# Every second product of a selective scan made on GpSimd, three units ahead, in a fused decoder kernel

## The chip, the cores and the metric

One core of one Trainium2 chip runs the whole kernel in one launch. The metric is device time in microseconds (us), from the start of the program to its end, median of several runs. Engines: TensorE (PE in the profile; PEld is its weight load), VectorE (DVE), ScalarE (ACT), GpSimd (POOL) and SyncE (SP), which here issues the DMAs.

## The reference, cut to what matters

Two decoder layers over 16 sequences of 256 tokens with 256 features, all float32: a Mamba block, a latent sparse attention and a quantised feed-forward net, then a self-attention, a cross-attention and a mixture of experts, each with a residual and a layer norm. The change is in the scan of the Mamba block (512 inner features, 16 states):

```
def step(h, inp):
    dt_t, B_t, C_t, x_t = inp
    dA = jnp.exp(dt_t[..., None] * A)
    dBx = dt_t[..., None] * B_t[:, None, :] * x_t[..., None]
    h = dA * h + dBx
    y_t = jnp.sum(h * C_t[:, None, :], axis=-1)
    return (h, y_t)
```

## The kernel before, in words

The scan of a sequence is cut into 32 units. A unit has 128 partitions (16 features by 8 states) and two halves of the states side by side, 128 x 512 elements for the 256 tokens. For unit k:

- SyncE loads two rows spread over the partitions from a scratch in HBM: dt into `dt_rep[k % 8]`, and dt*x into `dtx_rep[k % 8]` (L331). A buffer is loaded again when its reader of eight units before is done.
- ScalarE makes the decay exp(dt*A) into PSUM (L1061, two instructions). PSUM has room for two units, so decay k waits for scan k-2.
- The product dt*x*B goes into `hbuf[k % 8]`. This is the product of the title. VectorE makes it one unit ahead of its scan (L1515, B read from PSUM), or GpSimd does (L1314, B read from its copy `bsb` in SBUF).
- VectorE scans in place (L1535).
- GpSimd multiplies by C in place (L1322); call it multiplication k.
- TensorE sums over the states for four units at a time (L552), and with that four buffers come free (`y_ps`).

Before the change GpSimd makes products 3, 7, ..., 31, five units ahead, and VectorE the others. After the scan of a sequence GpSimd adds the convolution of the next one (L1302), three instructions for each half.

Each engine has two streams of pieces: the x stream (`all_first`: scan, latent attention, feed-forward net) of sequence i+1 and the y stream (`all_second`: self-attention, cross-attention, experts) of sequence i. `merged` weaves them in an order written out by hand in `ORDER`; each `yield` ends a piece. A number of x pieces goes ahead first, so the first sequence scans with nothing beside it. GpSimd has the scan's work and the convolution alone.

Neighbours of the scan in the y stream that the prediction speaks of: the layer norm (L1396, L1397 and L1398, 128x2 elements, and L1403 twice, 128x256) at the end of the experts, in front of scan 0, and again behind the self-attention, in front of scan 24; the projections (L745) and key copies (L1173) of self-attention; its row maxima (L1558) and score matmuls (L608, L627); the key projections (L770), key copies (L1183) and value projections (L780) of cross-attention; the last matmul of the experts (L860) with the first of the feed-forward net (L698).

The order in which GpSimd works, before:

```
product(3)
for k in range(UNITS):
    if k % 4 == 2 and k + 5 < UNITS:
        product(k + 5)
    pool.wait_ge(h_ready, at(i, UNITS, k + 1))
    nc.gpsimd.tensor_tensor(hbuf[k % HSLOTS], hbuf[k % HSLOTS],
                            csb, ALU.mult).then_inc(hc_ready, 1)
```

Of the kernel before, what the change touches and what calls it, by code (L numbers as in the profile page):

```python
# [51 lines left out]
def at(i, per, n):  # L52

    return i * per + n
# [65 lines left out]
def build(nc, dram, out):  # L120

    ctx = ExitStack()
    with ctx:
# [197 lines left out]
        def _(sp):  # L321
# [31 lines left out]
            def first_half(i):  # L353
# [10 lines left out]
                for k in range(UNITS):  # L364
# [10 lines left out]
                    if k == 4:  # L375
                        sp.wait_ge(cnt_ps, at(i, 4, 4))
                    if k >= SLOTS and k % 4 == 3:
                        sp.wait_ge(dbx_pool, at(i, UNITS // 4, (k - SLOTS) // 4 + 1))
                    elif k >= SLOTS:
                        sp.wait_ge(dbx, at(i, 24, (k - SLOTS) // 4 * 3 + k % 4 + 1))  # L380
                    if k == 0 or k == UNITS // 2:
# [9 lines left out]
                sp.wait_ge(decay_ready, at(i, UNITS, UNITS))  # L391
                sp.wait_ge(dbx, at(i, 24, 24))
                sp.wait_ge(dbx_pool, at(i, UNITS // 4, UNITS // 4))
                for row, name in ((fb1, "fb1"), (ln2g, "ln2g"), (ln2b, "ln2b")):
# [898 lines left out]
        def _(pool):  # L1293
# [11 lines left out]
            for i in range(B):  # L1305
                pool.wait_ge(c_sb, i + 1)

                def product(k):
                    if k == 3:
                        pool.wait_ge(dbx, at(i, 24, 1))  # L1310
                    elif k >= HSLOTS:
                        pool.wait_ge(y_ps, at(i, 8, k // 4 - 1))
                    pool.wait_ge(rep_dtx[k % SLOTS], at(i, 64, 16 * (k // SLOTS + 1)))
                    nc.gpsimd.tensor_tensor(hbuf[k % HSLOTS], dtx_rep[k % SLOTS].unsqueeze(1).to_broadcast([P, 2, T]), bsb,  # L1314
                                            ALU.mult).then_inc(dbx_pool, 1)

                product(3)
                for k in range(UNITS):
                    if k % 4 == 2 and k + 5 < UNITS:
                        product(k + 5)  # L1320
                    pool.wait_ge(h_ready, at(i, UNITS, k + 1))
# [6 lines left out]
        def _(v):  # L1328
# [154 lines left out]
            def mamba(i, c, before, dt_steps):  # L1483
# [25 lines left out]
                def product(k):  # L1509
                    if k % 4 == 3:  # L1510
                        return
# [10 lines left out]
                for k in range(UNITS):  # L1522
# [4 lines left out]
                    if k + 1 < UNITS:  # L1527
                        product(k + 1)
                        yield
                    if k % 4 == 3:  # L1530
                        v.wait_ge(dbx_pool, at(i, UNITS // 4, k // 4 + 1))
                    else:
                        v.wait_ge(dbx, at(i, 24, k // 4 * 3 + k % 4 + 1))
                    v.wait_ge(decay_ready, at(i, UNITS, k + 1))
# [339 lines left out]
```

## Time and profile before

| | |
|---|---|
| median of 3 runs | 3829.47 us (3828.81 to 3829.94) |
| profiled execution | 3828.33 us, its span 3826.5 us |
| TensorE busy | 3238.3 us (85%), weight loads 2244.7 (59%) |
| VectorE busy | 2824.9 us (74%) |
| ScalarE busy | 2083.5 us (54%) |
| GpSimd busy | 923.2 us (24%) |
| mean granted TensorE clock | 0.932 |

The span runs from the first to the last instruction of the program; the profiled execution's own time has 1.8 us more around it. Busy shares are averages over stages with different limits, so the timeline of a stage says more than they do. A row of the timeline gives start, duration, engine, line, operation, result and inputs with their shapes and the number of instructions put together (x2), and in brackets how long the engine stood idle before it and what ended that.

### The profile page before, as it was taken

The page shows a single profiled execution, that of the slowest core. Times are in us where ns is not written, and L with a number is a line of the kernel's source. Part 1 is how long each engine was busy: PE and PEld are TensorE (multiplying, and loading weights), DVE is VectorE, ACT ScalarE, POOL GpSimd, SP SyncE. Part 2 cuts the span into 40 slices and gives each one's busy share as a digit, 9 for nine tenths or more (in the row PEclk, how much of TensorE's full clock was granted, in tenths as well). Part 3 has the DMA queues.
Part 4 walks back from the last instruction along what each step waited for, and adds up shares of the span by engine and source line. Part 5 has one row for each costly group of instructions (what it writes and reads, how often), then busy time and mean ns, then how long its engine had stood idle before and what let it go on. Part 6 is the DMA issues. An engine that isn't in the chain of part 4 may idle for free.

```text
span 3826.5 us, 58993 instructions
## 1 busy us (share of the span) xinstructions
PE 3238.3 (85%) x22354; PEld 2244.7 (59%) x22402; DVE 2824.9 (74%) x4915; ACT 2083.5 (54%) x4816; POOL 923.2 (24%) x740
## 2 busy tenths in 40 slices
PE   2568989898898989889898998989889888988877
PEld 2245656666565666656556665656656566665655
DVE  4687786868778687777868778786877868687622
ACT  2356555565665556556564655656566565655432
POOL 1423050221404122150411305031230503124000
PEclk8679999999999999999999999999999999999988
DMA  5212041412304132140413215041320504132110
GB/s 185 81 60 93 24 142 48 144 70 80 134 15 149 51 135 79 54 157 17 149 51 127 87 41 170 17 145 56 123 91 31 168 29 139 61 114 94 47 42 17
DMA packets 205692, 336.50 MB, mean 88 GB/s; under 512 B 23968, under 2 KB 175008, under 8 KB 190688
## 3 DMA queue, kind: packets, MB, share of 16 engines
q1 hardware_dynamic: 205408, 332.72, 25.5%
q8 instruction: 177, 2.90, 0.3%
q14 instruction: 107, 0.88, 0.1%
HBM read 311.66 MB, written 20.97 MB: 87 GB/s over the span
## 4 chain that ended last, share of the span: by engine, by line
PE 60%; DVE 21%; ACT 13%; issue 5%; DMA 1%; SPq 0%; POOL 0%; DVEq 0%; ACTq 0%
PE ps L627 7%; PE ps L608 5%; PE ps L860 4%; PE ps L940 4%; DVE nm L1558 3%; PE ps L639 3%; PE ps L794 3%; PE ps L780 3%; PE ps L770 3%; PE ps L879 3%; PE ps L825 3%; PE ps L745 3%; PE ps L806 2%; PE ps L552 2%; PE ps L839 2%
## 5 line engine op out<-in xcount | busy, mean ns | idle before, releaser
L1322 POOL TENSOR_TENSOR region_x<-region_x 128x512 f32<-128x512 f32 x512 | 645.6, 1273 | 340.3 <-DVE region_x L1535 340.0
L1535 DVE TENSOR_TENSOR_SCAN region_x<-ps,region_x 128x512 f32<-128x512 f32 x512 | 614.8, 1214 | 68.6 <-ACT ps L1061 65.6
L1061 ACT ACTIVATE ps<-region_x,aneg 128x255 f32<-128x255 f32 x1024 | 441.7, 473 | 348.2 <-DVE region_x L1535 341.4
L1302 POOL TENSOR_TENSOR region_x<-region_x 128x512 f32<-128x512 f32 x96 | 122.5, 1276 | 1209.8 <-ACT region_x L1009 1204.8
L1314 POOL TENSOR_TENSOR region_x<-region_x 128x512 f32<-128x512 f32 x128 | 162.5, 1270 | 1030.7 <-DVE region_x L1515 894.2
L1558 DVE TENSOR_REDUCE nm<-ps 128x4 f32<-128x1024 f32 x256 | 308.8, 1222 | 65.8 <-PE ps L608 57.6
L879 PE MATMUL ps<-xTy,wide 128*128 128x256 f32 x1280 | 310.7, 391 | 1.5 <-DVE region_y L1722 1.3
L1210 ACT ACTIVATE region_y<-ps,rmax 128x256 f32<-128x256 f32 x512 | 236.0, 495 | 116.7 <-DVE rmax L1663 116.7
L1515 DVE TENSOR_TENSOR region_x<-region_x,ps 128x512 f32<-128x512 f32 x384 | 254.6, 667 | 20.5 <-PE ps L552 20.3
L879 PEld LDWEIGHTS ps<-xTy,wide 128*128 128x128 f32 x1280 | 237.6, 192 | 41.1 <-issue 8.7
L1571 DVE SCALAR_TENSOR_TENSOR region_x<-region_x,cntk 128x512 f32<-128x512 f32 x256 | 168.5, 690 | 114.6 <-ACT region_x L1102 114.6
L1663 DVE TENSOR_REDUCE rmax<-ps 128x4 f32<-128x1024 f32 x128 | 152.2, 1220 | 116.0 <-PE ps L806 116.0
L627 PE MATMUL ps<-region_y 64*128 64x256 f32 x1024 | 179.0, 477 | 64.2 <-ACT region_y L1102 35.8
L608 PE MATMUL ps<-region_y 64*128 64x256 f32 x1024 | 145.5, 412 | 74.3 <-DVE nm L1558 34.8
L1226 ACT ACTIVATE region_y<-ps 128x512 f32<-128x512 f32 x256 | 142.3, 599 | 103.2 <-PE ps L828 103.2
L552 PE MATMUL ps<-region_x,sely 128*32 128x256 f32 x2048 | 153.8, 429 | 47.6 <-POOL region_x L1322 47.6
L1102 ACT ACTIVATE region_x<-ps 128x512 f32<-128x512 f32 x256 | 145.3, 605 | 78.8 <-PE ps L627 78.7
L627 PEld LDWEIGHTS ps<-region_y 64*128 64x128 f32 x1024 | 106.1, 224 | 136.1 <-ACT region_y L1102 93.8
L1102 ACT ACTIVATE region_y<-ps 128x512 f32<-128x512 f32 x256 | 138.5, 593 | 75.3 <-PE ps L627 75.1
L1412 DVE TENSOR_TENSOR xh<-ps,xh 128x512 f32<-128x512 f32 x80 | 55.0, 687 | 160.6 <-PE ps L669 56.6
L608 PEld LDWEIGHTS ps<-region_y 64*128 64x128 f32 x1024 | 93.2, 194 | 126.6 <-DVE nm L1558 66.7
L975 ACT ACT_TABLE_LOAD x127 | 162.9, 1283 | 3.0 <-PEq L1864 0.7
(249 smaller groups left out, 6913.3 us busy)
## 6 DMA issues: line engine op xcount, KB each, us to landing
region_x<-rows_of_dt SPq DMA_DIRECT2D x1024, 128.0 KB, 2.9
wide<-in_wgate SPq DMA_DIRECT2D x16, 1280.0 KB, 7.2
wide<-in_wup SPq DMA_DIRECT2D x16, 1280.0 KB, 10.1
down<-in_wmoe SPq DMA_DIRECT2D x16, 1280.0 KB, 5.5
wide<-in_wq SPq DMA_DIRECT2D x16, 1024.0 KB, 7.0
wide<-in_wk SPq DMA_DIRECT2D x16, 1024.0 KB, 8.8
wide<-in_wv SPq DMA_DIRECT2D x16, 1024.0 KB, 10.6
down<-in_wo SPq DMA_DIRECT2D x16, 1024.0 KB, 13.2
```

The costliest lines, as they stand in the source:

```text
L552: last = mm(bank(0)[32 * j:32 * j + 32, m, :], W["sely"][:, e, :], hbuf[(4 * n + j) % HSLOTS][:, half, :], start=(e + half == 0), stop=(e ...
L608: last = mm(ps[:, b + j, qt * T:(qt + 1) * T], a.QT[r, t, qt * P:(qt + 1) * P], a.KT[u % 2][r, t, :], start=not a.masked, stop=not a.maske ...
L627: last = mm(ps[:, a.sT_bank(n + j), kt * T:(kt + 1) * T], a.KT[e][r, t, kt * P:(kt + 1) * P], a.QT[r, t, :], start=True, stop=True)
L879: last = mm(bank(b)[:, j, :], w[:, k, f * P:(f + 1) * P], xTy[:, k, :], start=(k == 0), stop=(k == KD - 1))
L1061: last = f(ps[:, 1 + 2 * (k % 2), half * T + 1:(half + 1) * T], dt_rep[k % SLOTS][:, 1:T], ACT.Exp, scale=aneg[:, k, half:half + 1])
L1102: f(a.PT[:, n % 8].rearrange("p k q -> p (k q)"), ps[:, a.sT_bank(n), :], ACT.Exp).then_inc(a.probs, 1)
L1210: last = f(junk2[:, 4 * (u % 2) + 2 * qt + g], ps[:, a.pair_bank(u) + g, qt * T:(qt + 1) * T], ACT.Exp, bias=rmax[:, qt, g, u:u + 1], accu ...
L1322: nc.gpsimd.tensor_tensor(hbuf[k % HSLOTS], hbuf[k % HSLOTS], csb, ALU.mult).then_inc(hc_ready, 1)
L1515: tt_(hbuf[k % HSLOTS], dtx_rep[k % SLOTS].unsqueeze(1).to_broadcast([P, 2, T]), bank(2), ALU.mult).then_inc(dbx, 1)
L1535: nc.vector.tensor_tensor_scan(flat(hbuf[k % HSLOTS]), ps[:, 1 + 2 * (k % 2), :], flat(hbuf[k % HSLOTS]), 0.0, ALU.mult, ALU.add).then_inc ...
L1558: last = nc.vector.tensor_reduce(at_nm[:, u % 2::2, :, 16 + t], ps[:, b:b + 2, :].rearrange("p g (q k) -> p g q k", k=T), AX, ALU.max, neg ...
L1571: stt(a.PT[:, n % 8], a.PT[:, n % 8], 4.0, cntk[:], ALU.min, ALU.mult).then_inc(a.weighed, 1)
```

## The change

GpSimd makes products 1, 3, 5, ..., 31 and VectorE products 0, 2, 4, ..., 30. GpSimd starts with product 1, and makes product k+3 in front of multiplication k for each even k. The counts behind the semaphores `dbx` (VectorE's products) and `dbx_pool` (GpSimd's) become 16 a sequence each, and SyncE's and VectorE's waits go by them. The order of pieces is the same; where VectorE has no product to make, its piece is empty.

```
--- before.py
+++ after.py
@@ -374,10 +374,10 @@
                     yield
                     if k == 4:
                         sp.wait_ge(cnt_ps, at(i, 4, 4))
-                    if k >= SLOTS and k % 4 == 3:
-                        sp.wait_ge(dbx_pool, at(i, UNITS // 4, (k - SLOTS) // 4 + 1))
+                    if k >= SLOTS and k % 2 == 1:
+                        sp.wait_ge(dbx_pool, at(i, UNITS // 2, (k - SLOTS) // 2 + 1))
                     elif k >= SLOTS:
-                        sp.wait_ge(dbx, at(i, 24, (k - SLOTS) // 4 * 3 + k % 4 + 1))
+                        sp.wait_ge(dbx, at(i, UNITS // 2, (k - SLOTS) // 2 + 1))
                     if k == 0 or k == UNITS // 2:
                         sp.wait_ge(dt_stored[1], at(i, 32, 16 if k == 0 else 32))
                     spread_rows(i, 1, k, dtx_rep[k % SLOTS]).then_inc(rep_dtx[k % SLOTS], 16)
@@ -389,8 +389,8 @@
                             load_x(i)
                 yield
                 sp.wait_ge(decay_ready, at(i, UNITS, UNITS))
-                sp.wait_ge(dbx, at(i, 24, 24))
-                sp.wait_ge(dbx_pool, at(i, UNITS // 4, UNITS // 4))
+                sp.wait_ge(dbx, at(i, UNITS // 2, UNITS // 2))
+                sp.wait_ge(dbx_pool, at(i, UNITS // 2, UNITS // 2))
                 for row, name in ((fb1, "fb1"), (ln2g, "ln2g"), (ln2b, "ln2b")):
                     sp.dma_start(row, dram[name]).then_inc(rows_loaded, 16)
                 yield
@@ -1306,18 +1306,18 @@
                 pool.wait_ge(c_sb, i + 1)
 
                 def product(k):
-                    if k == 3:
-                        pool.wait_ge(dbx, at(i, 24, 1))
+                    if k == 1:
+                        pool.wait_ge(dbx, at(i, UNITS // 2, 1))
                     elif k >= HSLOTS:
                         pool.wait_ge(y_ps, at(i, 8, k // 4 - 1))
                     pool.wait_ge(rep_dtx[k % SLOTS], at(i, 64, 16 * (k // SLOTS + 1)))
                     nc.gpsimd.tensor_tensor(hbuf[k % HSLOTS], dtx_rep[k % SLOTS].unsqueeze(1).to_broadcast([P, 2, T]), bsb,
                                             ALU.mult).then_inc(dbx_pool, 1)
 
-                product(3)
+                product(1)
                 for k in range(UNITS):
-                    if k % 4 == 2 and k + 5 < UNITS:
-                        product(k + 5)
+                    if k % 2 == 0 and k + 3 < UNITS:
+                        product(k + 3)
                     pool.wait_ge(h_ready, at(i, UNITS, k + 1))
                     nc.gpsimd.tensor_tensor(hbuf[k % HSLOTS], hbuf[k % HSLOTS],
                                             csb, ALU.mult).then_inc(hc_ready, 1)
@@ -1507,7 +1507,7 @@
                     tt_(yT[:, 2 * pair:2 * pair + 2, :], zs[:, 2 * pair:2 * pair + 2, :], y, ALU.mult).then_inc(y_done, 1)
 
                 def product(k):
-                    if k % 4 == 3:
+                    if k % 2 == 1:
                         return
                     v.wait_ge(rep_dtx[k % SLOTS], at(i, 64, 16 * (k // SLOTS + 1)))
                     if k >= HSLOTS and k % 4 == 0:
@@ -1527,10 +1527,10 @@
                     if k + 1 < UNITS:
                         product(k + 1)
                         yield
-                    if k % 4 == 3:
-                        v.wait_ge(dbx_pool, at(i, UNITS // 4, k // 4 + 1))
+                    if k % 2 == 1:
+                        v.wait_ge(dbx_pool, at(i, UNITS // 2, k // 2 + 1))
                     else:
-                        v.wait_ge(dbx, at(i, 24, k // 4 * 3 + k % 4 + 1))
+                        v.wait_ge(dbx, at(i, UNITS // 2, k // 2 + 1))
                     v.wait_ge(decay_ready, at(i, UNITS, k + 1))
                     nc.vector.tensor_tensor_scan(flat(hbuf[k % HSLOTS]), ps[:, 1 + 2 * (k % 2), :], flat(hbuf[k % HSLOTS]),
                                                  0.0, ALU.mult, ALU.add).then_inc(h_ready, 1)
```

## Rows read from the trace of the kernel before

**Rows 1.** The page's chain that ended last, shares of the span by engine.

```profile
PE 60%; DVE 21%; ACT 13%; issue 5%; DMA 1%; SPq 0%; POOL 0%; DVEq 0%; ACTq 0%
```

**Rows 2.** The page's groups of products: count, busy us, mean ns, idle before.

```profile
L1314 POOL TENSOR_TENSOR region_x<-region_x 128x512 f32<-128x512 f32 x128 | 162.5, 1270 | 1030.7 <-DVE region_x L1515 894.2
...
L1515 DVE TENSOR_TENSOR region_x<-region_x,ps 128x512 f32<-128x512 f32 x384 | 254.6, 667 | 20.5 <-PE ps L552 20.3
```

**Rows 3.** Timeline of the first sequence's scan, GpSimd and TensorE.

```profile
87.63 1.27 POOL L1314 TENSOR_TENSOR region_x<-region_x 128x512 f32<-128x512 f32 x1 [19.69 <-DMA region_x<-rows_of_dt]
88.86 2.49 POOL L1322 TENSOR_TENSOR region_x<-region_x 128x512 f32<-128x512 f32 x2
...
94.62 4.95 POOL L1322 TENSOR_TENSOR region_x<-region_x 128x512 f32<-128x512 f32 x4
...
141.17 1.93 PE L552 MATMUL ps<-region_x,sely 128*32 128x256 f32 x16 [3.08 <-POOL region_x L1322]
```

**Rows 4.** Timeline of VectorE beside the convolution adds of GpSimd.

```profile
1774.63 3.96 POOL L1302 TENSOR_TENSOR region_x<-region_x 128x512 f32<-128x512 f32 x3 [72.44 <-ACT region_x L1009]
...
1775.01 0.92 DVE L1396 SCALAR_TENSOR_TENSOR x_nt<-x_mv,x_rstd 128x2 f32<-128x2 f32 x1 [0.24 <-ACT x_rstd L988]
...
1781.48 0.29 DVE L1431 TENSOR_SCALAR region_x<-region_x 128x256 bf16<-128x256 f32 x1
...
1782.40 1.34 DVE L1431 TENSOR_SCALAR region_x<-region_x 128x256 bf16<-128x256 f32 x1
```

**Rows 5.** Timeline of the start of the ninth sequence's scan, GpSimd and VectorE.

```profile
1847.10 1.27 POOL L1314 TENSOR_TENSOR region_x<-region_x 128x512 f32<-128x512 f32 x1 [60.76 <-DVE region_x L1515]
...
1847.48 0.90 DVE L1396 SCALAR_TENSOR_TENSOR y_nt<-y_mv,y_rstd 128x2 f32<-128x2 f32 x1
...
1848.81 0.74 DVE L1403 TENSOR_SCALAR xh<-xh,y_mv,y_rstd 128x256 f32<-128x256 f32 x2
...
1849.46 1.22 DVE L1535 TENSOR_TENSOR_SCAN region_x<-ps,region_x 128x512 f32<-128x512 f32 x1
```

**Rows 6.** Timeline in front of the key copies L1173.

```profile
1854.25 3.62 PE L745 MATMUL ps<-xTy,wk 128*128 128x256 f32 x16
...
1857.02 0.87 ACT L1061 ACTIVATE ps<-region_x,aneg 128x255 f32<-128x255 f32 x2 [0.84 <-DVE region_x L1535]
...
1857.91 3.76 ACT L1173 ACTIVATE region_y<-ps,kbp,hmp 128x256 f32<-128x256 f32 x8
```

**Rows 7.** The chain among the row maxima: start, us, what.

```profile
1867.17 0.68 DVE region_x L1515
```

**Rows 8.** Timeline around the second layer norm, in front of scan 24.

```profile
1907.91 2.50 POOL L1322 TENSOR_TENSOR region_x<-region_x 128x512 f32<-128x512 f32 x2
...
1910.44 0.16 DVE L1396 SCALAR_TENSOR_TENSOR y_nt<-y_mv,y_rstd 128x2 f32<-128x2 f32 x1
...
1913.00 0.87 ACT L1061 ACTIVATE ps<-region_x,aneg 128x255 f32<-128x255 f32 x2 [1.33 <-DVE region_x L1535]
...
1913.81 1.06 ACT L1183 ACTIVATE region_y<-ps 128x512 f32<-128x512 f32 x2
...
1914.68 0.30 PEld L780 LDWEIGHTS ps<-wide,ctxT 128*128 128x128 f32 x2 [0.41 <-ACT region_y L1183]
```

**Rows 9.** Timeline: first scans of the 14th and 15th sequence.

```profile
2976.12 1.22 DVE L1535 TENSOR_TENSOR_SCAN region_x<-ps,region_x 128x512 f32<-128x512 f32 x1
...
3201.14 1.22 DVE L1535 TENSOR_TENSOR_SCAN region_x<-ps,region_x 128x512 f32<-128x512 f32 x1
```

**Rows 10.** Timeline of TensorE at L860, in two sequences.

```profile
1783.98 6.10 PE L860 MATMUL ps<-down,region_y 128*128 128x256 f32 x16
1790.14 1.67 PE L698 MATMUL ps<-w1q,region_x 128*128 128x512 bf16 x7
...
2009.12 6.17 PE L860 MATMUL ps<-down,region_y 128*128 128x256 f32 x16
2015.35 1.67 PE L698 MATMUL ps<-w1q,region_x 128*128 128x512 bf16 x7
```

More of the change, by code:

```diff
@@ L376, in first_half @@
                         sp.wait_ge(cnt_ps, at(i, 4, 4))
-                    if k >= SLOTS and k % 4 == 3:
-                        sp.wait_ge(dbx_pool, at(i, UNITS // 4, (k - SLOTS) // 4 + 1))
+                    if k >= SLOTS and k % 2 == 1:
+                        sp.wait_ge(dbx_pool, at(i, UNITS // 2, (k - SLOTS) // 2 + 1))
                     elif k >= SLOTS:
-                        sp.wait_ge(dbx, at(i, 24, (k - SLOTS) // 4 * 3 + k % 4 + 1))
+                        sp.wait_ge(dbx, at(i, UNITS // 2, (k - SLOTS) // 2 + 1))
                     if k == 0 or k == UNITS // 2:
@@ L391, in first_half @@
                 sp.wait_ge(decay_ready, at(i, UNITS, UNITS))
-                sp.wait_ge(dbx, at(i, 24, 24))
-                sp.wait_ge(dbx_pool, at(i, UNITS // 4, UNITS // 4))
+                sp.wait_ge(dbx, at(i, UNITS // 2, UNITS // 2))
+                sp.wait_ge(dbx_pool, at(i, UNITS // 2, UNITS // 2))
                 for row, name in ((fb1, "fb1"), (ln2g, "ln2g"), (ln2b, "ln2b")):
@@ L1308, in product @@
                 def product(k):
-                    if k == 3:
-                        pool.wait_ge(dbx, at(i, 24, 1))
+                    if k == 1:
+                        pool.wait_ge(dbx, at(i, UNITS // 2, 1))
                     elif k >= HSLOTS:
@@ L1315, in product @@
                                             ALU.mult).then_inc(dbx_pool, 1)
-                product(3)
+                product(1)
                 for k in range(UNITS):
-                    if k % 4 == 2 and k + 5 < UNITS:
-                        product(k + 5)
+                    if k % 2 == 0 and k + 3 < UNITS:
+                        product(k + 3)
                     pool.wait_ge(h_ready, at(i, UNITS, k + 1))
@@ L1509, in product @@
                 def product(k):
-                    if k % 4 == 3:
+                    if k % 2 == 1:
                         return
@@ L1529, in mamba @@
                         yield
-                    if k % 4 == 3:
-                        v.wait_ge(dbx_pool, at(i, UNITS // 4, k // 4 + 1))
+                    if k % 2 == 1:
+                        v.wait_ge(dbx_pool, at(i, UNITS // 2, k // 2 + 1))
                     else:
-                        v.wait_ge(dbx, at(i, 24, k // 4 * 3 + k % 4 + 1))
+                        v.wait_ge(dbx, at(i, UNITS // 2, k // 2 + 1))
                     v.wait_ge(decay_ready, at(i, UNITS, k + 1))
```

## The prediction

> **What bounds the kernel now.** I read the chain that ended last first. TensorE has 60% of it, VectorE 21%, ScalarE 13%, GpSimd 0% [rows 1]. So moving VectorE work to GpSimd can gain only where VectorE is on that chain, and can lose where GpSimd or what it disturbs gets onto it. The groups then give the prices: a product costs 667 ns on VectorE and 1270 ns on GpSimd [rows 2], a scan 1.22 us [rows 5]. Products and scans of one unit after another start closer together than that; I use 0.57 to 0.60 us as what a product takes out of VectorE's time where neighbours overlap.
>
> The timeline shows two regimes. The first sequence scans alone, and there GpSimd works almost without a pause; TensorE's last sum at 141.17 waits for it [rows 3]. From the second sequence on, the scan of one sequence is woven with the attention of the sequence before, and everything repeats: from the first scan at 1849.46 to that at 3201.14 are 1351.68 us, which is six times 225.28 us [rows 5, 9].
>
> **The change part by part.** Products 1, 5, ..., 29 of each sequence go from VectorE to GpSimd: 8 x 16 = 128 instructions. VectorE loses 128 x 0.667 = 85 us of work, GpSimd gains 128 x 1.270 = 163 us [rows 2]. Every product on GpSimd now stands three units ahead of its scan instead of five. SyncE's waits before the row loads follow the products; those of the moved products come no later than before, so I cost them at nothing, hidden by the eight row buffers; with that cover gone each load would add its 2.9 us.
>
> First sequence. Before, GpSimd starts the first multiplication by C at 88.86, behind product 3 [rows 3]. After, products 1 and 3 are both done by then, since product 3 starts at 87.63 only because its rows land then. What is left from 88.86 is 32 multiplications and 14 products, 46 instructions. Back to back they start 1.227 us apart (four took 4.95: (4.95 - 1.27) / 3) [rows 3]. 88.86 + 46 x 1.227 = 145.3, against 141.1 where TensorE's last sum starts now. VectorE's two units take at most 3.1 us then (two scans and one product: 2 x 1.22 + 0.67), GpSimd's 3.68, so GpSimd is the bound and its products are what the scans wait for. Loss: 4.2 us, all of it on the chain, since nothing else runs in this sequence. Bounds: 0, if later work of the sequence hid it; 5.5 with one more product of 1.27 exposed.
>
> Beginning of each later sequence. A small VectorE instruction that reads two tensors from SBUF waits while GpSimd runs an instruction: beside the convolution adds of GpSimd the 128x2 operation L1396 took 0.92 us, and of two equal tensor_scalar operations, L1431, one took 0.29 us and the next 1.34 [rows 4]; with GpSimd idle L1396 takes 0.16 [rows 8]. At the start of the scan the last layer norm of the other sequence (L1396 to L1403) is followed by scan 0. Before, L1396 already waits for product 3 on GpSimd: 0.90 us, and ends at 1848.38, with GpSimd's instruction [rows 5]. After, GpSimd runs products 1 and 3 one behind the other, from 1847.1 to 1849.6, so one of these small operations waits for the first and another for the second. With L1403 (0.74 us for the pair) still to come, scan 0 starts at about 1850.35 instead of 1849.46: 0.9 us late, though VectorE has a product less before it. No row shows L1403 beside a busy GpSimd; I let it wait, by the row of L1431. If it doesn't wait, scan 0 is not late, which is the other bound. The skill says which VectorE instructions are meant: by the Trainium skill, GPSIMD Engine Reference, section 8 (Key points), the two engines share their SBUF interfaces, and those in a 2-port mode or with two SBUF inputs contend. By it the scan and the product, which each read PSUM and one SBUF tensor, pay nothing for the 128 new neighbours.
>
> The delay goes on to ScalarE: scans 0 to 4 release decay 6, behind which the key copies L1173 are queued. Without product 5 the path from scan 0 is 0.57 shorter. Decay 6 ended at 1857.89, TensorE's own input to L1173 came at 1857.87, and L1173 started at 1857.91 [rows 6]: both paths are full. After: 0.9 - 0.57 = +0.33 us on the chain (bounds 0 and 0.9; a gain is excluded, since TensorE's 1857.87 does not move).
>
> Row-maximum stretch. Here eight row maxima (L1558) share VectorE with the scans. At 1867.17 product 9 stands in the chain with 0.68 us [rows 7]. It goes: -0.58 us (bounds -0.68 and 0). GpSimd has it long before scan 9, which comes some 9 us behind it.
>
> Second layer norm. Units 20 to 23: GpSimd ran multiplications 22 and 23 from 1907.91 to 1910.41, then stood idle, and L1396 started at 1910.44 and took 0.16 [rows 8]. After, product 25 takes the place of 27 in front of these two, and product 27 starts behind them at 1910.4, before multiplication 24. L1396 or L1397 waits for it until 1911.65: scan 24 starts 1.05 us late. ScalarE's decay 26 waits for scan 24 (1913.00, idle 1.33 for VectorE), and the key copies L1183 are queued behind it. TensorE's value projection L780 at 1914.68 waits for these copies [rows 8]. They were ready at 1914.4 and come 1.05 later, TensorE goes on about 0.73 us late (bounds 0 and 1.1). From there to the sequence's end the chain is on TensorE. The other moved products (13, 17, 21) leave VectorE where it then waits for ScalarE or TensorE: nothing.
>
> Sum for one later sequence: +0.33 - 0.58 + 0.73 = +0.48 us.
>
> **What the repetition does with it.** It need not add up. The first scan at 2976.12 came 0.26 us behind the beat (1849.46 + 5 x 225.28 = 2975.86), the next sequence's, at 3201.14, stood exactly on it [rows 9]: a delay was given back within one sequence. The rows show one place where: L860 started at 1783.98, which is 0.14 behind its place by the next sequence (2009.12 - 225.28 = 1783.84), and L698 behind it at 1790.14 only 0.07 behind (2015.35 - 225.28 = 1790.07) [rows 10]. This happens in a stretch at the lower of TensorE's clocks (16 multiplications took 6.1 us): what starts later has less of its work left in it. A standing extra of 0.48 a sequence is absorbed in the same way, and only a standing lag of some 0.5 to 0.9 us is left at the end. I take 0.6.
>
> Forecast: 4.2 + 0.6 = 4.8 us. The profiled execution had 3828.33 us around a span of 3826.5; that gives 3833.1. Its time is 1.1 below the median of 3829.47, so a median of 3834.3; I say 3834. The change is 0.12%, and a measurement of this kernel can tell about 0.2% (7.7 us) from no change.
>
> **Rivals.**
> - The extra is not given back (slower). 15 x 0.48 = 7.2, with 4.2 it makes 11.4: 3841, +0.3%. It decides from 0.24 us a sequence on. For it: each term has its row. Against: rows 9. Chance 0.22.
> - The small operations wait no longer than now, and product 9's time counts each time: 4.2 - 15 x 0.58 = -4.5, 3825. For it: L1403's wait is shown by no row. Against: two products in a row are longer than one. Chance 0.14.
> - TensorE's first stretch at the lower clock falls elsewhere and VectorE's path is freed of products 1, 5 and 9: 4.2 - 15 x (0.58 + 1.15) = -21.8, 3808. For it: the lag moves TensorE's work. Against: L1173 also has ScalarE's path, full as it is. Chance 0.08.
> - GpSimd becomes the bound in every sequence, as in the first: 16 x 4.2 = 67, 3897. Against: in the later ones it stands idle in between, as from 1910.41 until scan 24 is done [rows 8]. Chance 0.07. The Trainium skill, GPSIMD Engine Reference, section 4.1 (Engine selection), speaks for this one, since it sends elementwise work on tiles to VectorE and calls GpSimd about twice as slow with two inputs; the rows agree on the ratio (1270 to 667).
> - The forecast, around 3834 (3828 to 3838): 0.49.
>
> **How the numbers follow.** Faster by over 0.2%: the third rival and the edge of the second, 0.1. Slower: the first, the fourth and the forecast's edge, 0.3. The same: 0.6. The range leaves out the third and fourth and reaches from below the second to behind the first with its bounds (15 x 0.9 = 13.5 with the 4.2): 3820 to 3847.
>
> **What would show it.** Right: in the first sequence the last L1322 ends near 145.3 and has next to no idle time; 256 products on each engine; L1396 to L1403 at the start of a scan together about 0.9 us longer; L1396 or L1397 near scan 24 at 1.1 to 1.3 us; sequences still 225.28 us apart. Wrong: another distance between sequences, which multiplies by 15, or stretches at the lower clock in other places; or L1535 waiting for L1314.

## The result, and the profile after

The changed kernel took 3855.64 us (median of 4, 3853.51 to 3857.13), the kernel before 3829.14 us (median of 4): ratio 1.0075, 95% interval 1.0063 to 1.0086. It is 0.75% slower. The forecast was 3834, with a range up to 3847: the measured time lies behind the range, and a difference that this measurement tells from none was forecast as one that it could not. The profiled execution had 3853.51 us around a span of 3851.5.

The page, chain by engine and four of its groups (line, engine, operation, count; busy us, mean ns; idle time before, and what ended it):

```profile
span 3851.5 us, 59089 instructions
...
PE 59%; DVE 20%; ACT 13%; issue 5%; POOL 1%; SPq 0%; DMA 0%; DVEq 0%; ACTq 0%
...
L1535 DVE TENSOR_TENSOR_SCAN region_x<-ps,region_x 128x512 f32<-128x512 f32 x512 | 610.3, 1210 | 99.6 <-ACT ps L1061 97.2
...
L1314 POOL TENSOR_TENSOR region_x<-region_x 128x512 f32<-128x512 f32 x256 | 324.9, 1271 | 1002.7 <-DVE region_x L1515 916.2
...
L627 PE MATMUL ps<-region_y 64*128 64x256 f32 x1024 | 193.7, 510 | 62.3 <-ACT region_y L1102 33.9
...
L1515 DVE TENSOR_TENSOR region_x<-region_x,ps 128x512 f32<-128x512 f32 x256 | 170.2, 665 | 28.3 <-PE ps L552 28.0
```

The work moved as foreseen: 256 products on each engine, 128 fewer on VectorE, each at its old price [rows 2]. The chain's shares are nearly those of [rows 1]; GpSimd has only 1% of it. Of the 99.6 us that VectorE stands idle ahead of its scans (L1535), 97.2 end with ScalarE's decay and next to none with GpSimd's products. So neither more work nor a new bound explains 25 us.

The timeline, first scans of the ninth, 14th and 15th sequence (start us, us, what):

```profile
1861.11 1.21 DVE L1535 TENSOR_TENSOR_SCAN region_x<-ps,region_x 128x512 f32<-128x512 f32 x1
...
2996.11 1.21 DVE L1535 TENSOR_TENSOR_SCAN region_x<-ps,region_x 128x512 f32<-128x512 f32 x1
...
3223.02 1.21 DVE L1535 TENSOR_TENSOR_SCAN region_x<-ps,region_x 128x512 f32<-128x512 f32 x1
```

From 1861.11 to 3223.02 are 1361.91 us, six times 226.99, where [rows 5, 9] had six times 225.28. That is the loss. From the end of TensorE's last instruction of the experts (L940) in the first sequence (491.85 before and after to 0.03) to the same in the 14th, the kernel now needs 2952.31 us instead of 2929.06; the rest behind it is 1.74 longer: 23.25 + 1.74 = 25.0 us of span.

**First sequence.** GpSimd, then TensorE's last sum:

```profile
85.35 1.26 POOL L1314 TENSOR_TENSOR region_x<-region_x 128x512 f32<-128x512 f32 x1 [0.80 <-DMA region_x<-rows_of_dt]
86.57 2.49 POOL L1322 TENSOR_TENSOR region_x<-region_x 128x512 f32<-128x512 f32 x2
...
143.23 1.93 PE L552 MATMUL ps<-region_x,sely 128*32 128x256 f32 x16 [4.18 <-POOL region_x L1322]
```

The rate was right: 86.57 + 46 x 1.227 = 143.0. The first multiplication stands 2.3 us earlier than in [rows 3], of which 1.9 is the start of this execution: SyncE's first stores of dt (L325) stand at 76.03 against 77.95, ahead of anything that the change touches. So TensorE's last sum is 2.06 us late, and 4.0 against its own start (forecast 4.2). At the end of the first sequence's experts both executions stand at the same place.

**Start of a later scan.** The same place as [rows 5]:

```profile
1858.01 0.15 DVE L1396 SCALAR_TENSOR_TENSOR y_nt<-y_mv,y_rstd 128x2 f32<-128x2 f32 x1
1858.20 0.16 DVE L1397 SCALAR_TENSOR_TENSOR y_nt<-y_nt,y_rstd 128x2 f32<-128x2 f32 x1
1858.23 2.49 POOL L1314 TENSOR_TENSOR region_x<-region_x 128x512 f32<-128x512 f32 x2 [60.62 <-DVE region_x L1515]
...
1858.39 1.12 DVE L1398 SCALAR_TENSOR_TENSOR y_rstd<-y_nt,y_rstd 128x2 f32<-128x2 f32 x1
...
1859.55 1.64 DVE L1403 TENSOR_SCALAR xh<-xh,y_mv,y_rstd 128x256 f32<-128x256 f32 x2
...
1861.11 1.21 DVE L1535 TENSOR_TENSOR_SCAN region_x<-ps,region_x 128x512 f32<-128x512 f32 x1
```

VectorE comes free 0.60 us earlier now (2.83 us behind the last instruction of the experts, 1844.05 before and 1855.18 after, instead of 3.43), because the product for unit 1 is gone, and slips L1396 and L1397 in ahead of GpSimd. Then L1398 waits for product 1 (1.12 instead of 0.16) and L1403 for product 3 (1.64 instead of 0.74). Measured from the end of the previous sequence's experts, scan 0 is 0.52 us late. The 0.9 forecast had the right mechanism with the wrong starting point.

**Second layer norm.** The same place as [rows 8]:

```profile
1919.22 2.49 POOL L1322 TENSOR_TENSOR region_x<-region_x 128x512 f32<-128x512 f32 x2
...
1921.68 1.27 POOL L1314 TENSOR_TENSOR region_x<-region_x 128x512 f32<-128x512 f32 x1
1921.77 1.20 DVE L1396 SCALAR_TENSOR_TENSOR y_nt<-y_mv,y_rstd 128x2 f32<-128x2 f32 x1 [0.60 <-ACT y_rstd L988]
...
1922.98 0.41 PEld L780 LDWEIGHTS ps<-wide,ctxT 128*128 128x128 f32 x2
```

L1396, a 128x2 operation, takes 1.20 us beside product 27. Scan 24 is 1.04 us late and TensorE's L780 0.79 (forecast 1.05 and 0.73).

**What nobody had forecast.** TensorE's granted clock by stretch (us, PE busy, PEclk), before and then after. The first two stretches of each are the scores L627; the third is a 32 us piece of the experts:

```profile
1881.06:1887.89 6.83, 6.01 (x36) 0.50 0.41 119
1887.89:1891.30 3.41, 2.77 (x30) 1.00 0.51 169
2026.00:2058.00 32.00, 31.79 (x265) 1.00 0.15 49
```

```profile
1888.66:1895.49 6.83, 4.81 (x20) 0.50 0.19 64
1895.49:1898.90 3.41, 3.41 (x26) 0.50 0.57 181
2036.00:2068.00 32.00, 31.16 (x234) 0.95 0.11 41
```

0.50 is the level of 1.2 GHz, 1.00 that of 2.4. Ahead of both stretches TensorE works on row maxima's scores (L608) and stands in front of each pair. Before, the clock falls at 1881.06, 2.2 us behind the first L627 at 1878.85; after, it falls at 1888.66, ahead of the first at 1889.32, and stays down for 10.24 us. So the early L627 groups run at half rate:

```profile
1889.32 2.08 PE L627 MATMUL ps<-region_y 64*128 64x256 f32 x8 [1.80 <-DVE region_y L1566]
1892.07 2.08 PE L627 MATMUL ps<-region_y 64*128 64x256 f32 x8 [0.68 <-ACT region_y L1102]
1894.83 2.08 PE L627 MATMUL ps<-region_y 64*128 64x256 f32 x8 [0.68 <-ACT region_y L1102]
```

where the kernel before had 1.13, 1.73 and 2.08. In every second sequence a further stretch at 1.2 GHz, of 3.41 us, falls into the experts, where TensorE was busy for 31.79 of 32.00 us before the change.

Two neighbouring sequences together (marks against the end of the previous experts) account for the 3.4 us: L780 late 0.78 + 0.79; L627 1.15 + 0.80; experts 1.40; row maxima without product 9 -0.65 and -0.06; smaller shifts +0.09; and L860, which gives back 0.54 and 0.20. The sum is 3.56 us against one sequence of the kernel before that took 225.21; against two average ones of 225.28 it is 3.56 - 2 x 0.07 = 3.42, 1.71 a sequence.

### The profile page after: what moved, and what is told of

The parts are those of the page before. It is cut to its first block, busy times and chain, and to the rows that moved or that the text cites. A ratio compares the mean times of both kernels' runs of the same rounds, so it can differ in the third digit from the quotient of the medians.

```text
span 3851.5 us, 59089 instructions
## 1 busy us (share of the span) xinstructions
PE 3260.5 (85%) x22354; PEld 2259.0 (59%) x22402; DVE 2783.6 (72%) x4787; ACT 2083.6 (54%) x4816; POOL 1077.2 (28%) x868
## 4 chain that ended last, share of the span: by engine, by line
PE 59%; DVE 20%; ACT 13%; issue 5%; POOL 1%; SPq 0%; DMA 0%; DVEq 0%; ACTq 0%
PE ps L627 8%; PE ps L879 6%; PE ps L608 6%; PE ps L940 4%; PE ps L860 4%; DVE region_x L1535 3%; PE ps L639 3%; PE ps L794 3%; DVE nm L1558 3%; PE ps L825 3%; PE ps L806 2%; PE ps L780 2%; PE ps L745 2%; PE ps L839 2%; PE ps L604 2%
## 5 line engine op out<-in xcount | busy, mean ns | idle before, releaser
L1322 POOL TENSOR_TENSOR region_x<-region_x 128x512 f32<-128x512 f32 x512 | 645.8, 1274 | 242.0 <-DVE region_x L1535 240.8
L1535 DVE TENSOR_TENSOR_SCAN region_x<-ps,region_x 128x512 f32<-128x512 f32 x512 | 610.3, 1210 | 99.6 <-ACT ps L1061 97.2
L1314 POOL TENSOR_TENSOR region_x<-region_x 128x512 f32<-128x512 f32 x256 | 324.9, 1271 | 1002.7 <-DVE region_x L1515 916.2
L1302 POOL TENSOR_TENSOR region_x<-region_x 128x512 f32<-128x512 f32 x96 | 122.5, 1276 | 1207.3 <-ACT region_x L1009 1202.3
L879 PE MATMUL ps<-xTy,wide 128*128 128x256 f32 x1280 | 324.1, 403 | 1.7 <-DVE region_y L1722 1.3
L879 PEld LDWEIGHTS ps<-xTy,wide 128*128 128x128 f32 x1280 | 246.6, 199 | 45.9 <-issue 8.7
L627 PE MATMUL ps<-region_y 64*128 64x256 f32 x1024 | 193.7, 510 | 62.3 <-ACT region_y L1102 33.9
L608 PE MATMUL ps<-region_y 64*128 64x256 f32 x1024 | 153.6, 437 | 61.5 <-DVE VP L1648 31.8
L627 PEld LDWEIGHTS ps<-region_y 64*128 64x128 f32 x1024 | 114.0, 241 | 139.9 <-ACT region_y L1102 95.6
L1515 DVE TENSOR_TENSOR region_x<-region_x,ps 128x512 f32<-128x512 f32 x256 | 170.2, 665 | 28.3 <-PE ps L552 28.0
L608 PEld LDWEIGHTS ps<-region_y 64*128 64x128 f32 x1024 | 100.4, 207 | 114.7 <-DVE nm L1558 53.3
## 6 DMA issues: line engine op xcount, KB each, us to landing
wide<-in_wup SPq DMA_DIRECT2D x16, 1280.0 KB, 10.2
```

What stands on the lines that cost most here:

```text
L608: last = mm(ps[:, b + j, qt * T:(qt + 1) * T], a.QT[r, t, qt * P:(qt + 1) * P], a.KT[u % 2][r, t, :], start=not a.masked, stop=not a.maske ...
L627: last = mm(ps[:, a.sT_bank(n + j), kt * T:(kt + 1) * T], a.KT[e][r, t, kt * P:(kt + 1) * P], a.QT[r, t, :], start=True, stop=True)
L879: last = mm(bank(b)[:, j, :], w[:, k, f * P:(f + 1) * P], xTy[:, k, :], start=(k == 0), stop=(k == KD - 1))
L1322: nc.gpsimd.tensor_tensor(hbuf[k % HSLOTS], hbuf[k % HSLOTS], csb, ALU.mult).then_inc(hc_ready, 1)
L1515: tt_(hbuf[k % HSLOTS], dtx_rep[k % SLOTS].unsqueeze(1).to_broadcast([P, 2, T]), bank(2), ALU.mult).then_inc(dbx, 1)
L1535: nc.vector.tensor_tensor_scan(flat(hbuf[k % HSLOTS]), ps[:, 1 + 2 * (k % 2), :], flat(hbuf[k % HSLOTS]), 0.0, ALU.mult, ALU.add).then_inc ...
```

## The experiments

Sixteen kernels, in four groups (e1 to e4); each group has its own runs of the kernel before, with medians of 3825.94, 3828.24, 3825.31 and 3826.82 us, and the ratio is taken to those. "Distance" is the mean from one sequence's last L940 to the next one's over ten sequences (4th to 14th) of the profiled execution; a distance that keeps coming back I call a beat. To move single products, the kernels hold GpSimd's order in a list of (unit, multiplication, b for ahead or a for behind):

```
+PLAN = [(1, -1, "b"), (3, 0, "b"), (5, 2, "b"), ..., (27, 24, "b"), (29, 26, "b"), (31, 28, "b")]
...
-                    if k % 2 == 0 and k + 3 < UNITS:
-                        product(k + 3)
+                    products(k, "b")
                     pool.wait_ge(h_ready, at(i, UNITS, k + 1))
                     nc.gpsimd.tensor_tensor(hbuf[k % HSLOTS], hbuf[k % HSLOTS],
                                             csb, ALU.mult).then_inc(hc_ready, 1)
+                    products(k, "a")
```

| kernel | us | ratio to before (95%) | distance | low clock, us a sequence |
|---|---|---|---|---|
| before | 3829.14 | | 225.28 | 19.8 |
| changed | 3855.64 | 1.0075 (1.0063 to 1.0086) | 226.99 | 25.6 |
| e1_27 | 3831.30 | 1.0013 (1.0003 to 1.0022) | 225.29 | 23.9 |
| e1_start | 3826.45 | 1.0003 (0.9993 to 1.0012) | 225.28 | 22.5 |
| e1_late24 | 3854.27 | 1.0074 (1.0059 to 1.0089) | 227.49 | 24.9 |
| e1_only9 | 3827.32 | 1.0000 (0.9991 to 1.0010) | 225.28 | 23.9 |
| e2_both | 3826.89 | 0.9993 (0.9984 to 1.0003) | 225.28 | 23.9 |
| e2_split | 3827.43 | 0.9993 (0.9984 to 1.0002) | 225.28 | 23.9 |
| e2_both10 | 3827.42 | 0.9994 (0.9984 to 1.0004) | 225.28 | 27.3 |
| e2_half24 | 3839.28 | 1.0024 (1.0014 to 1.0034) | 225.80 | 21.2 |
| e3_fill | 3934.06 | 1.0282 (1.0264 to 1.0299) | 232.00 | 5.8 |
| e3_fill_after | 3942.00 | 1.0299 (1.0284 to 1.0315) | 232.09 | 4.1 |
| e3_fill_both | 3940.42 | 1.0297 (1.0282 to 1.0312) | 232.02 | 5.8 |
| e3_fill_late | 3938.40 | 1.0293 (1.0278 to 1.0308) | 232.07 | 3.8 |
| e4_fill | 3852.79 | 1.0068 (1.0053 to 1.0083) | 226.99 | 10.2 |
| e4_fill_after | 3853.36 | 1.0077 (1.0062 to 1.0092) | 226.84 | 8.2 |
| e4_fill_both | 3831.69 | 1.0017 (1.0007 to 1.0026) | 225.63 | 7.5 |
| e4_light | 3839.21 | 1.0030 (1.0017 to 1.0043) | 227.04 | 13.7 |

Two rows need care. The profiled execution of e4_fill_after took 3864.45 us, its other three 3852.36 to 3853.68, so its distance (five sequences of 228.7, then 225.4 to 228.1) is not that of the median. In e4_light the first sequence's experts end at 484.37 us instead of 491.88, which hides part of its longer distance in the time.

### Which delay makes the loss

**e1_27**, the changed kernel with product 27 behind multiplication 24:

```
-(27, 24, "b")
+(27, 24, "a")
```

> The changed kernel, but product 27 made behind multiplication 24 and not in front of it, so that it does not run beside the layer norm ahead of scan 24. Theory A (the port wait at scan 24 makes TensorE 0.79 us late in every sequence, and TensorE's low-clock stretches turn that into 1.7 us a sequence): L1396 to L1398 there take 0.16 us each again, L780 is on time, the distance between sequences goes back from 227.0 to about 225.3 us, the time to 3826 to 3832. Theory B (the terms simply add, the clock does nothing of its own): 15 x 0.79 = 12 us less than the changed kernel, 3844. Theory C (GpSimd's doubled load in the dense units is what costs): no more than 3 us less, 3852 or above.

The layer norm is free again (the kernel's lines are numbered three to eight higher):

```profile
1910.66 2.49 POOL L1329 TENSOR_TENSOR region_x<-region_x 128x512 f32<-128x512 f32 x2
...
1913.20 0.16 DVE L1404 SCALAR_TENSOR_TENSOR y_nt<-y_mv,y_rstd 128x2 f32<-128x2 f32 x1 [0.60 <-ACT y_rstd L991]
...
1914.44 1.22 DVE L1543 TENSOR_TENSOR_SCAN region_x<-ps,region_x 128x512 f32<-128x512 f32 x1
```

The distance is back at 225.29, though scan 0 is still 0.52 late, and the time is what theory A gave (B: 3844, C: 3852 or above). Moving one of 16 products by one place takes back all but some 5 us of the loss.

**e1_start**, the changed kernel with product 1 on VectorE again:

```
-PLAN = [(1, -1, "b"), (3, 0, "b"), (5, 2, "b"), ...
+PLAN = [(3, -1, "b"), (5, 2, "b"), ...
```

> The changed kernel, but product 1 back on VectorE, so that GpSimd has one product beside the layer norm ahead of scan 0, as before the change. Theory A: scan 0 comes 0.5 us earlier, but the key copies L1173 start with TensorE's weights-side input anyway and do not move; the term at scan 24 stays, so the time stays at 3852 to 3858. Theory B: no change either, within 2 us. If the start of the scan were what breaks the beat, the time would fall to 3830 or so.

A miss for the theory that the wait at scan 24 alone makes the loss. Product 27 still stands beside the layer norm here, yet the distance is 225.28. TensorE starts the key projections (L770) 1.3 us early, so that L780 is 0.5 early in spite of the wait; by the end of the experts this gain is gone (+0.09). Either edit cures the loss: neither wait makes it alone.

**e1_late24**, the kernel before with a VectorE reduction over constants in front of scan 24, its result unused:

```
+                    if k == 24:
+                        nc.vector.tensor_reduce(spare[:, 12:13], W["win"][:, 0, :], AX, ALU.max)
```

> The kernel before, with one idle-making VectorE instruction (a maximum over 1024 constants, about 1.2 us, whose result nothing reads) put in front of scan 24, and nothing else changed: the delay of scan 24 by itself. Theory A: TensorE's L780 late by about 0.9 us each time, and low-clock stretches grow, so that the time is 3848 to 3860, more than the plain sum. Theory B: 15 x 0.9 = 14 us, 3843. If delays are given back as the prediction had it: 3830. Theory C: nothing above 3832.

```profile
1923.93 1.21 DVE L1544 TENSOR_REDUCE spare<-win 128x1 f32<-128x1024 f32 x1
```

No product has moved here. Scan 24 is 1.13 late, L780 0.9, and the kernel is as slow as the changed one (1.0074 against 1.0075). So a delay of 0.9 us in front of L780 is enough for 1.7 us and more a sequence. GpSimd's part in the loss is only that it made such a delay. The time is in theory A's range (3848 to 3860), above B's plain sum of 3843.

**e1_only9**, the kernel before with product 9 alone on GpSimd:

```
-PLAN = [(3, -1, "b"), (7, 2, "b"), (11, 6, "b"), ...
+PLAN = [(3, -1, "b"), (7, 2, "b"), (9, 6, "b"), (11, 6, "b"), ...
```

> The kernel before, with product 9 alone moved to GpSimd (in front of multiplication 6, with product 11 behind it as before): only the part of the change that takes 0.6 us out of VectorE's chain among the row maxima. Theory A: the distance between sequences either stays at 225.28 us (3829, the gain is taken back by the low-clock stretches) or falls to a shorter beat. Theory B: 15 x 0.59 = 9 us faster, 3820.

The row maxima end 0.64 us earlier, as in [rows 7], but scan 15 is 0.52 late: L627 meets a stretch of 10.24 us at 1.2 GHz instead of 6.83. The distance stays 225.28 (theory B's 3820 did not come). A gain of 0.6 us is taken back as well.

### How much is given back, on either side

**e2_both**, both cures together (product 1 on VectorE, 27 behind multiplication 24); **e2_split**, product 1 on GpSimd, product 3 behind multiplication 0, and 27 behind 24; **e2_both10**, e2_both with product 10 on GpSimd too; **e2_half24**, e1_late24 with 512 elements:

```
e2_both     +PLAN = [(3, -1, "b"), (5, 2, "b"), ..., (27, 24, "a"), ...
e2_split    +PLAN = [(1, -1, "b"), (3, 0, "a"), (5, 2, "b"), ..., (27, 24, "a"), ...
e2_both10   +PLAN = [(3, -1, "b"), ..., (9, 6, "b"), (10, 7, "b"), (11, 8, "b"), ..., (27, 24, "a"), ...
e2_half24   -tensor_reduce(spare[:, 12:13], W["win"][:, 0, :], AX, ALU.max)
            +tensor_reduce(spare[:, 12:13], W["win"][:, 0, 0:512], AX, ALU.max)
```

> The changed kernel without either port wait: product 1 back on VectorE, product 27 behind multiplication 24. By the marks of the runs with one of the two, TensorE's L794 ends 0.5 - 0.8 = 1.3 us nearer to the sequence's start than before the change. Theory A (a beat that only jumps): the distance between sequences stays at about 225.3 us and the time at 3822 to 3830, or it jumps to the next shorter beat, some 1.7 us less for each sequence: 3798 to 3806. Theory B (terms add): 15 x 1.3 = 20 us less than before, 3806.

> As the run before, but product 1 stays on GpSimd and product 3 goes behind multiplication 0, so that one GpSimd product stands beside the layer norm ahead of scan 0 and VectorE has one product less. Theory A: L1398 waits for product 1 (1.1 us), L1403 for nothing (0.74 for the pair), scan 0 comes within 0.3 us of its place of before; the time is within 3 us of the run before. Theory B: 15 x 0.3 us or less apart from it.

> As e2_both, and product 10, the other product among the row maxima, goes to GpSimd too (in front of multiplication 7). VectorE's chain there gets another 0.6 us shorter, 1.9 us in all. Theory A: this is over the 1.7 us between two beats, so that the jump to the shorter beat comes: 3798 to 3806. Theory B: 15 x 1.9 = 28 us, 3798 as well. If the beat holds at 225.28 us: 3822 to 3830.

> The kernel before with a delay of half the size in front of scan 24 (a maximum over 512 constants, about 0.65 us, of which TensorE gets some 0.4). Theory A: this stays below the jump, the distance between sequences stays at 225.28 us, the time at 3826 to 3831. Theory B (proportional to e1_late24, which had 28 us for about 0.9 us at TensorE): 12 us slower, 3838 to 3842.

e2_both and e2_split have sequences of 223.7 and 226.9 us in turn: 225.28 on average. In e2_both10 the distance is again 225.28 each time, with 27.3 us of low clock a sequence, the most of all: neither theory's 3798 came. Its scan 5 is 0.60 early, but scan 8, inside a low-clock stretch that the kernel before does not have there, is 0.83 late. Where VectorE has less to do, TensorE runs more of its work at 1.2 GHz. No version with all waits cured is measurably faster than the kernel before (0.9993, interval up to 1.0003). e2_half24 shows the other edge: for five sequences in a row it holds 225.28 with L780 0.27 late, ahead of them and behind them L780 is up to 1.6 late and a sequence takes 226.8 to 227.3. Its 3839.28 misses theory A (3826 to 3831) and lies where B had it (3838 to 3842), but not as B meant: its ten executions spread from 3829.18 to 3845.50, where those of e1_late24 lie within 1.5 us of one another, and in the profiled one no distance is 0.8 us longer, as a plain share of 12 us would make it: five hold the beat, two lie 0.1 and 0.3 above it, six 1.5 to 2.0.

### Is it the clock that keeps the distance?

**e3_fill**: the kernel before with multiplications nobody reads, put on TensorE where it stands idle ahead of its low-clock stretches (L687 are transposes of the feed-forward net, L614 those ahead of L627). **e3_fill_after**, **e3_fill_both**, **e3_fill_late**: the same on the changed kernel, e2_both and e1_late24. One of the places:

```
+            def filler(count, where, w=None, **flags):
+                for _ in range(count):
+                    mm(where, W["win"][:, 0, 0:P] if w is None else w, W["win"][:, 0, 0:T], **(flags or dict(start=True, stop=True)))
...
+                if not a.masked and i + 1 < B:
+                    filler(6, bank(0)[:, 1, :])
                 pe.wait_ge(a.shifted, i + 1)
```

> The kernel before with matrix multiplications whose result nobody reads, put on TensorE in front of the waits behind which its low-clock stretches come: 11 and 5 ahead of the two transposes of L687, 8 ahead of L745, 18 ahead of the pairs of L608, 2 ahead of L614 and 6 ahead of L627 of y, each 0.22 us at the 2.4 GHz level, together 11 us in the 14 us in which TensorE stood there. In the kernel before each sequence has three low-clock stretches of 6.83 us. Theory A (the distance of 225.28 us between sequences is kept by where the clock falls): the stretches at L687, L745 and L627 go or move, the granted clock rises from 0.93 to over 0.96, the distance leaves 225.28 us and falls by 3 to 10 us, the time to between 3670 and 3790 us. Theory B (the clock is a bystander, the distance is that of the waits): the clock rises but the distance stays within 0.5 us of 225.28, the time within 10 us of the kernel before. If the clock does not rise, the run tells nothing between them.

> The changed kernel with the same multiplications that nobody reads. Theory A: with the low-clock stretches gone the change costs what its waits cost, the later start of the scan and multiplication 24 (0.5 to 1 us a sequence): 8 to 16 us above the kernel before with the same filler, not 26. Theory B: 24 to 28 us above it, as without filler.

> The changed kernel with product 1 back on VectorE and product 27 behind multiplication 24 (the version whose sequences came out at 225.3 us on average though its row maxima were 0.6 us and its start 0.7 us earlier), with the same filler. Theory A: the gain that the low clock took back shows: 6 to 20 us below the kernel before with filler. Theory B: within 4 us of it.

> The kernel before with the reduce of 1024 constants ahead of scan 24 (1.1 us, which alone cost 26 us) and with the same filler. Theory A: it costs what its delay is, at most 0.9 us a sequence: 6 to 15 us above the kernel before with filler. Theory B: 24 to 30 us above it.

The filler cost 0.43 us each, not 0.22 (each stands in the trace as two matmul instructions), and eight of them stood behind the wait ahead of L745. So both theories missed e3_fill's time; it went up to 232.00 us a sequence. The comparison among the four can still be read. Between 1650 and 3200 us (behind the length: TensorE's busy time, its instructions, and PEclk), in the kernel before, the changed kernel, e3_fill and e3_fill_after:

```profile
1650.00:3200.00 1550.00, 1370.07 (x9660) 0.96 0.26 88
```

```profile
1650.00:3200.00 1550.00, 1374.74 (x9562) 0.94 0.26 87
```

```profile
1650.00:3200.00 1550.00, 1442.85 (x9987) 0.99 0.27 91
```

```profile
1650.00:3200.00 1550.00, 1436.67 (x9975) 0.99 0.27 91
```

With nearly all at 2.4 GHz, L780 is still 0.79 later in e3_fill_after than in e3_fill (7.35 against 6.56 us behind its place in the kernel before), and in e3_fill_late 0.88. Yet the distances are 232.00 and 232.09: the loss of 1.7 us a sequence is gone, and of the 0.79 us 0.09 are left. The waits do not swallow it. Through all that runs at 2.4 GHz the delay neither grows nor shrinks: it is still 0.81, on average over the ten sequences, at the start of the experts' matmuls (L879; L893 in the filled kernels). There it vanishes, and there the last stretches at 1.2 GHz stand. One sequence, e3_fill and then e3_fill_after:

```profile
2077.53 7.11 PE L893 MATMUL ps<-xTy,wide 128*128 128x256 f32 x24
```

```profile
2084.05 5.43 PE L893 MATMUL ps<-xTy,wide 128*128 128x256 f32 x24
```

The same 24 instructions take 1.68 us less where no low-clock stretch meets them. A stretch of 3.41 us stands there in seven of ten sequences of e3_fill and in two of e3_fill_after: (7 - 2) x 1.7 / 10 = 0.85 us a sequence, which is what vanishes. So even here it is the clock that gives the delay back, as it made more of it in the changed kernel.

The 7.9 us between the two kernels' medians (theory A: 8 to 16, B: 24 to 28) arise mostly outside the beat. Of the 9.3 us between the profiled spans 6.67 stand at the end of the first sequence's experts (502.66 instead of 495.99), 0.57 in the 13 distances and 2.07 behind them. The place of that first mark varies from 484 to 503 us among these kernels, also where no product has moved (498.45 in e3_fill_late), and I have no cause for it. e3_fill_late stands 4.3 us above e3_fill (A: 6 to 15, B: 24 to 30). For e3_fill_both A expected a gain; it was 6.4 slower, a miss for both.

**e4_fill** and the rest repeat it with a filler cut to TensorE's idle time, 30 a sequence (the expectations say 28, but the groups that they list add up to 30, and the trace has 60 instructions of them), those ahead of L745 in front of its wait; **e4_light** has 14:

```
-                    filler((11, 5)[tt], bank(2)[:, 0, :])
+                    filler((7, 3)[tt], bank(2)[:, 0, :])
...
-                        filler((0, 6, 1, 2, 3, 2, 2, 2)[u], bank(0)[:, 0, :], zpad[:], start=False, stop=False)
+                        filler((0, 4, 1, 1, 2, 1, 1, 1)[u], bank(0)[:, 0, :], zpad[:], start=False, stop=False)
...
                 last.then_inc(S.xT_ps, 1)
+                filler(fill, bank(0)[:, 1, :])
                 pe.wait_ge(S.xT_ready, nth)
```

> The kernel before with multiplications that nobody reads, 28 a sequence at 0.43 us, each group no longer than the idle time of TensorE that it is put into: 7 and 3 ahead of the transposes of L687 (3.30 and 1.68 us idle), 4 ahead of the wait for x transposed (2.26), 4, 1, 1, 2, 1, 1, 1 inside the pairs of L608, 1 ahead of L614, 4 ahead of L627 (1.80). They add nothing to TensorE's path. Theory A (the low clock keeps the distance): the three low-clock stretches become fewer or shorter, as in e3_fill, and the distance leaves 225.28 us downwards, by 3 to 10 us a sequence: 3680 to 3790 us at a granted clock over 0.95. Theory B (the distance is that of the waits, the clock follows): 225 us a sequence and 3820 to 3840 us even at the higher clock.

> The changed kernel with the same fitted filler. Theory A: not 26 us above e4_fill; the distance is either the same as in e4_fill (then 0 to 12 us above, from the first sequences) or the next one that holds. Theory B: 24 to 28 us above e4_fill.

> The changed kernel with product 1 on VectorE and product 27 behind multiplication 24, with the same fitted filler. In e3_fill_both nothing came through, its path led over TensorE. Here the shorter row maxima (0.6 us) can shorten the distance only if VectorE ends last there: 0 to 10 us below e4_fill by theory A, within 4 us of it by theory B.

> The kernel before with 14 such multiplications a sequence instead of 28 (4 and 2 at L687, 2 ahead of x transposed, 4 in the pairs of L608, 2 ahead of L627). Theory A: between: at least one of the three low-clock stretches stays, clock 0.935 to 0.96, 3750 to 3829 us. Theory B: 3820 to 3835 us.

e4_fill is a miss for both theories. Its low clock is halved (10.2 us a sequence instead of 19.8), its L745 ends 2.95 us earlier, and it is 26 us slower than the kernel before. Its distance of 226.99 is that of the changed kernel, with quite different work in it. Part of the cost is the filler's, which did not stay off TensorE's path as expected: scan 9 is 1.9 to 2.4 us late, L780 1.3 to 1.5. Part is where the clock now falls:

```profile
2032.23:2039.06 6.83, 6.83 (x21) 0.50 0.01 2
```

In these 6.83 us, at the start of the experts, TensorE is busy all the time, so that half rate costs its full price; the stretch at 1881.06 of the kernel before had 0.82 us without work in it, and waits for other engines around it. From the end of L860 to L940 this sequence goes from 1.26 us early to 2.50 late against the kernel before. The changed kernel with this filler is only 0.6 us above e4_fill (A: 0 to 12, B: 24 to 28), and e4_fill_both 21 us below it (A: 0 to 10, B: within 4), at 225.63 us a sequence. e4_light is at 3839, a miss for both (A: 3750 to 3829, B: 3820 to 3835).

One relation in the traces goes further. The common low-clock stretch is 6.83 us long (6.827 to one more digit), the shorter one of 3.41 half of it. The beat of 225.28 us is 33 times 6.827. Two sequences of the changed kernel, of e4_fill and of e4_light (453.98 us each, where they have settled) are 66.5 times it, and three of e1_late24 (682.66 where they repeat) 100 times. So after one, two or three sequences the stretches can meet the same work again. In the changed kernel they start in two layouts that alternate, 2.8, 33.5, 163.2 and 183.7 us behind the end of the experts and 4.4, 21.5, 35.1 and 164.8. In e3, with little of the low clock left, the ratio holds only roughly (four sequences take 927.1 to 929.7 us; 136 times 6.827 is 928.5), and e2_half24, e4_fill_after and e4_fill_both, whose distances don't settle, show none.

What follows. Shown: the loss of the change is not the sum of its delays; a delay of 0.9 us in front of L780 costs 1.7 us and more a sequence in the kernel before, and 0.1 in the kernels of e3, where a low-clock stretch that no longer comes gives it back; in the changed kernel what is lost beyond the delay stands in work that meets a stretch at 1.2 GHz (L627, and the experts); equal distances (225.28 as the mean of six kernels, 232.0 to 232.1 of four) come out of different work. Shown too: more of the low clock does not mean a longer time (27.3 us a sequence in e2_both10 at 3827, 10.2 in e4_fill at 3853). Argued, not shown: that the clock's stretches pick the beat. The whole ratios speak for it, and so does that in e1_only9, e2_both10 and e3_fill_after the gain or the delay was undone inside one of them. Why a kernel settles at 226.99 rather than 225.28 or 227.49 is left open beyond that; no run here holds the clock at one level throughout.

## Why the prediction was wrong, step by step

- **What bounds it, and the number and price of products**: right.
- **First sequence, +4.2**: 4.0 against its own start at TensorE's last sum, so the term is right; 2.06 on the clock, since this execution began 1.9 us earlier. Behind the experts it is 0 here and 1.2 in e1_27, whose first scan is all but the same: some of it is given back on the way, as the lower bound had it.
- **Beginning of each later scan, 0.9**: 0.52; the path to L1173, forecast +0.33, came out at -0.16 to -0.06. e1_start puts the wait's whole effect at more than that: without product 1, L1173 starts 0.67 earlier. I had excluded a gain there because TensorE's input at 1857.87 would not move; it moved, since the clock rose sooner behind L745.
- **Row maxima, -0.58**: -0.59 from scan 5 to scan 8 in every second sequence, and nothing in the others.
- **Second layer norm, +1.05 and +0.73**: 1.04 and 0.79. The rule of the Trainium skill, GPSIMD Engine Reference, section 8 (Key points), fits the trace: scan and product stayed at 1.21 and 0.67 us beside 128 more neighbours. L1403, with one tensor input in SBUF, waited as well (1.64 instead of 0.74); the page would count it in if it ran in a 2-port mode, which no trace names.
- **The sum, +0.48**: by the measured terms (-0.1 at L1173, -0.3 on average at the row maxima, +0.79) about +0.4. Nothing wrong here.
- **"What the repetition does with it"** is the step that failed. "A standing extra of 0.48 a sequence is absorbed in the same way": I had seen one delay of 0.26 us given back at L860 [rows 9, 10] and carried it over to an extra that comes back every time and is larger where it matters (0.79 at L780, not 0.48). L860 did give back 0.2 to 0.5. But the same shift brought the clock's fall ahead of the first L627 (1.95 us in two sequences) and, every second time, into the experts (1.40). The 0.48 was neither absorbed (+4.8 in all) nor added up (+11.4, the first rival) but tipped the kernel into another beat: 1.7 x 15 = 25 us.
- **Rivals**: the first had the sign and not the size. The second did not come: the small operations waited longer, L1403 too. The third, a low-clock stretch that falls elsewhere, had the mechanism, but I priced it only as a gain. The fourth, GpSimd as the bound everywhere, didn't come about. What I had named as the sign of a wrong prediction, another distance between sequences, is what the trace shows.

The Trainium skill, TensorE: Matmul & The Clock Gate, section "HAM oscillation — how this bites in real kernels", advises for thin matmuls that wait on DMA to restructure the loop so that TensorE's clock stays up. Here the clock was kept up by other means, and in e4_fill it was up for longer (10.2 instead of 19.8 us low a sequence) and the time was 26 us longer.

## What to carry to other kernels

In a loop whose distance repeats to a few hundredths of a us although its trace holds stretches at TensorE's lower clock, do not add up terms of a few tenths: test how much delay and how much gain the distance swallows, with one instruction of no use put on the path (e1_late24, e2_half24) and one taken off (e1_only9). Here it swallowed gains of 0.6 us (measured) up to some 1.9 (the sum expected of e2_both10) and a delay of 0.3, and a delay of 0.9 us cost more than twice its size. When work is moved to GpSimd, look first at which small VectorE operations stand beside it, and place each instruction in a gap: one product moved by one place was worth about 24 us here.

## What the runs showed of the hardware

- A VectorE operation on 128x2 elements that meets a GpSimd product (1.27 us) waits nearly all of it: 1.12 and 1.20 us instead of 0.16. A tensor_scalar on 128x256 waits as well (pair 1.64 instead of 0.74).
- Ahead of L745 and L627 TensorE's granted clock fell to 0.50 although no idle time there was longer than 2.3 us, and a stretch at the low clock can hold nothing but work (6.83 of 6.83 us).
- A float32 multiplication 128x128 by 128x256 took 0.43 us of TensorE at 2.4 GHz, two instructions of 0.22 in the trace.
